# Stage 4 attention of a perceiver-style decoder: scores, transposes and values in another order, normalisation moved to the output copy, and spare products in the waits of the norms

## The reference, cut to what matters

```python
q = (query @ Wq + bq).reshape(b, -1, H, HD).transpose(0, 2, 1, 3)     # b=8, 64 tokens, H=16, HD=32
k = (key @ Wk + bk).reshape(b, -1, H, HD).transpose(0, 2, 1, 3)       # key = value = ctx, 1601 rows
v = (value @ Wv + bv).reshape(b, -1, H, HD).transpose(0, 2, 1, 3)
scores = jnp.einsum('bhsd,bhtd->bhst', q, k) / sqrt(HD)
scores = jnp.where(keep[None, None], scores, neg)
w = jax.nn.softmax(scores, axis=-1)
w = jnp.where(keep[None, None], w, 0)
out = jnp.einsum('bhst,bhtd->bhsd', w, v)
return out.transpose(0, 2, 1, 3).reshape(b, -1, D) @ Wo + bo
```

## Time and profile before

| what | us |
|---|---|
| median of 3 runs | 3006.52 (3006.23 to 3009.16) |
| the profiled execution, its own time | 3007.62 |
| its span in the trace | 3005.7 |
| PE busy in that span | 2785.7 (93%) |
| DVE busy | 1232.9 (41%) |
| ACT busy | 987.7 (33%) |

### The profile page before, as it was taken

One profiled execution on the slowest core, in us unless ns is written; L12 is line 12 of the kernel. 1 busy time (PEld: TensorE's weight loads), 2 busy tenths in 40 slices (PEclk: granted clock), 3 DMA queues, 4 the chain that ended last, 5 costly groups with the idle time before them and its releaser, 6 DMA issues.

```text
span 3005.7 us, 40740 instructions
## 1 busy us (share of the span) xinstructions
PE 2785.7 (93%) x17928; PEld 1966.6 (65%) x17928; DVE 1232.9 (41%) x1873; ACT 987.7 (33%) x1484; POOL 287.2 (10%) x278
## 2 busy tenths in 40 slices
PE   8979999998899799999999969999999999988698
PEld 3347346456587478888888838778778878853433
DVE  4364343447731633333333342442443343344612
ACT  3243113125342344344334412432332332331210
POOL 1110110221012000000000011011011001000000
PEclk9999999998899999999999979999999999999799
DMA  8964994951021132222222210100100100013198
GB/s 358 356 235 151 377 355 174 382 187 52 15 98 56 57 113 99 98 98 98 98 98 94 92 70 22 42 18 34 47 26 22 47 26 22 26 64 126 43 396 359
DMA packets 61967, 385.52 MB, mean 128 GB/s; under 512 B 6192, under 2 KB 10544, under 8 KB 32352
## 3 DMA queue, kind: packets, MB, share of 16 engines
q1 hardware_dynamic: 27072, 190.58, 16.7%
q0 software_dynamic: 29776, 188.15, 16.3%
q10 hardware_dynamic: 4944, 4.20, 0.4%
HBM read 377.64 MB, written 5.26 MB: 127 GB/s over the span
## 4 chain that ended last, share of the span: by engine, by line
PE 77%; DVE 8%; DMA 3%; ACT 3%; issue 1%; POOL 1%; ACTq 0%; DVEq 0%; POOLq 0%
PE PS L431 11%; PE PS L432 11%; PE PS L433 11%; PE PS L310 4%; PE PS L1859 3%; PE PS L1840 3%; PE PS L631 3%; PE PS L1823 3%; PE PS L1842 3%; PE PS L1841 3%; PE PS L1824 3%; PE PS L1825 3%; PE PS L1876 3%; PE PS L604 2%; DMA PR<-in_ctxN 2%; DVE T L1329 2%
## 5 line engine op out<-in xcount | busy, mean ns | idle before, releaser
L431 PE MATMUL PS<-X_high,W_high 128*128 128x512 f32 x576 | 226.5, 393 | 11.0 <-DVE X_low L1240 11.0
L431 PE MATMUL PS<-H_high,W_high 128*128 128x512 f32 x576 | 224.8, 390 | 2.1 <-DVE rstd L1545 2.1
L432 PE MATMUL PS<-X_low,W_high 128*128 128x512 f32 x576 | 225.8, 392 | 0.0
L433 PE MATMUL PS<-X_high,W_part 128*128 128x512 f32 x576 | 225.5, 392 | 0.0
L432 PE MATMUL PS<-H_low,W_high 128*128 128x512 f32 x576 | 224.8, 390 | 0.0
L433 PE MATMUL PS<-H_high,W_part 128*128 128x512 f32 x576 | 224.6, 390 | 0.0
L1187 DVE TENSOR_TENSOR W_part<-ring,W_high 128x2048 fp32r<-128x2048 f32 x63 | 147.1, 2334 | 185.0 <-ACT W_high L1183 185.0
L1183 ACT ACTIVATE W_high<-ring 128x2048 fp32r<-128x2048 f32 x72 | 137.0, 1914 | 252.4 <-PE PS L433 252.4
L2025 DVE TENSOR_TENSOR RB<-PS,rows 128x512 f32<-128x512 f32 x104 | 71.9, 691 | 312.8 <-PE PS L1842 312.8
L1226 DVE TENSOR_TENSOR H_low<-T,H_high 128x512 fp32r<-128x512 f32 x144 | 99.4, 691 | 210.5 <-ACT H_high L1213 210.5
L1955 ACT ACTIVATE RC<-PS,vec 128x384 f32<-128x384 f32 (+2 forms) x128 | 76.3, 596 | 322.4 <-PE PS L1825 322.4
(11 more groups left out here) (380 smaller groups left out, 5490.5 us busy)
## 6 DMA issues: line engine op xcount, KB each, us to landing
ring<-in_experts SPq DMA_DIRECT2D x83, 1024.0 KB, 4.8
ring<-in_tiles SPq DMA_DIRECT2D x39, 1024.0 KB, 4.9
RC<-in_ctxN POOLq DMA_DIRECT2D x24, 1536.0 KB, 12.3
RA<-in_ctxT POOLq DMA_DIRECT2D x20, 1536.0 KB, 7.2
T<-in_ctxN POOLq DMA_DIRECT2D x24, 1024.0 KB, 16.2
RA<-in_ctxT POOLq DMA_DIRECT2D x12, 1666.0 KB, 14.1
RB<-in_ctxT POOLq DMA_DIRECT2D x12, 1666.0 KB, 15.6
RB<-in_ctxT POOLq DMA_DIRECT2D x12, 1536.0 KB, 10.6
```

The lines of the kernel that those rows point to most:

```text
L431: pe.matmul(ps, a, xh, start=start, stop=False)
L432: pe.matmul(ps, a, xl, start=False, stop=False)
L433: return pe.matmul(ps, b, xh, start=False, stop=stop)
```

## The change

It has two parts. In stage 4: the scores of a group take 4 x 448 columns that overlap (0 to 447, 768 to 1215; 320 to 767, 1216 to 1663) rather than 4 x 416; the keys of the second half are made with the key weights' columns turned by 64 (`wrapped_high`, `wrapped_low`, bias `bk4s`) and a second copy of the queries turned likewise (`QSB`), so that the two products of a head over two column ranges lie in different strips of rows. Which heads form a group changes, and the rows of Wo are permuted to match. `normalise` is gone; `inverse` writes reciprocals of the sums, repeated 32 times, into a 128 x 128 tile, which one product with `FOLD` (L1939) spreads into PSUM behind the last two transposed blocks; the copy of the group's output multiplies by it and by `flag`. Transposes are cut into 7 pieces (6 of 4 blocks, one of 2 blocks and the product). Scores, transposes and values stand in another order, and three of the 8 units of the next batch's first keys stand inside groups 2 and 3. In the norms from stage 2 on: `turn_over` issues bf16 products of 128 x 512 whose result nobody reads, 5 behind the mean, 5 (14 in one place) behind the squares, and 10 or 22 behind the last spread.

```diff
+        def turn_over(pe, at, n, k=7):
+            pe.wait_ge(*at.done("idb"))
+            if bank_reader.get(k):
+                pe.wait_ge(*at.done(bank_reader[k]))
+            for _ in range(n):
+                pe.matmul(bank(k), idb[:, :], constants, start=True, stop=True)
...
-        def norm_pe(pe, at, tag, x, after):
+        def norm_pe(pe, at, tag, x, after, n=10):
 
             norm_mean(pe, at, tag, x, after)
+            turn_over(pe, at, 5)
             norm_squares(pe, at, tag, TS[5])
+            turn_over(pe, at, 5)
             norm_scale(pe, at, tag)
+            turn_over(pe, at, n)
...
+                for p in (0, 1):
+                    if g or h:
+                        pe.wait_ge(*at.done(f"{N}.m{g}.0.{p}" if h else f"{N}.m{g - 1}.1.{p}"))
+                    for late, m in enumerate(scored(h)):
+                        for u in (0, 1):
+                            block = 4 * (g // 2) + 2 * u + g % 2
+                            place = (block - late) % 8
+                            r = slice(place % 2 * S + p * HD, place % 2 * S + (p + 1) * HD)
+                            mm = pe.matmul(PS[u * S:(u + 1) * S, 2 * p + late, 0:SW], (QSB if late else QS)[r, place // 2, :], KT[r, place // 2, m:m + SW],
+                                           start=True, stop=True)
+                    mm.then_inc(*at.step(f"{N}.S{g}.{h}.{p}"))
...
                 for g in range(KC):
-                    transposes(b, g, 0, 0)
-                    transposes(b, g, 0, 1)
-                    transposes(b, g, 1, 0)
-                    transposes(b, g, 1, 1)
-                    if g + 1 < KC:
+                    if g in (1, 2):
                         scores(b, g + 1, 1)
+                    transposes(b, g, 0, 1, 2, 3)
                     values(b, g, 0)
-                    transposes(b, g, 2, 0)
-                    transposes(b, g, 2, 1)
-                    values(b, g, 1)
-                    transposes(b, g, 3, 0)
-                    transposes(b, g, 3, 1)
-                    values(b, g, 2)
-                    if g + 2 < KC:
-                        scores(b, g + 2, 0)
-                    if g + 1 == KC and b + 1 < B:
-                        keys(b + 1, 0)
-                    values(b, g, 3)
+                    if g == 0:
+                        scores(b, 1, 1)
+                    elif g == 1:
+                        scores(b, 3, 0)
+                    elif b + 1 < B:
+                        keys(b + 1, 0, range(g - 2, g - 1))
+                    transposes(b, g, 4, 5, 6)
+                    if g == 3 and b + 1 < B:
+                        keys(b + 1, 0, range(2, 3))
+                    values(b, g, 1, 2, 3)
+                    if g == 0:
+                        scores(b, 2, 0)
+                if b + 1 < B:
+                    keys(b + 1, 0, range(3, 8))
...
-            def normalise(b, g, q):
-                x, sm = prob[2 * (g % 2) + q], total4[g % 2][q]
-                dve.wait_ge(*at.done(f"s4.{b}.exp{g}.{q}"))
-                dve.reciprocal(sm, sm).then_inc(*at.step())
-                dve.wait_ge(*at.own())
-                dve.tensor_scalar(x, x, sm, flag, ALU.mult, ALU.mult).then_inc(*at.step(f"s4.{b}.p{g}.{q}"))
+            def inverse(b, g):
+                dve.wait_ge(*at.done(f"s4.{b}.exp{g}.1"))
...
+                for u in (0, 1):
+                    r = slice(u * S, (u + 1) * S)
+                    dve.reciprocal(INV[r, :, u, :], total4[g % 2][r, :].unsqueeze(2).broadcast_to([S, 2, HD])).then_inc(*at.step(f"s4.{b}.inv{g}"))
```

More of the change, by code:

```diff
@@ L1648, in s3_pe @@
             linear_pe(pe, at, "s3.o", [("s3.wo", O3)], (0, 1, 2, 3), range(KC), ["s3.at.O3.out"])
-            norm_pe(pe, at, "s3.ln1", X3, [f"s3.o.{c}.out" for c in range(KC)])
+            norm_pe(pe, at, "s3.ln1", X3, [f"s3.o.{c}.out" for c in range(KC)], 22)
             def gates_turned():
@@ new lines, in transposes @@
+            def transposes(b, g, *pieces):
+                N = f"s4.{b}"
+                for i in pieces:
+                    s = g * PN + i
+                    if s >= 3:
+                        due = [f"{N}.t{s - 3}.out"]
+                    elif s < 2:
+                        due = [f"{N}.V1.{HALF[1][1] - 1 - s}.out"]
+                    else:
+                        due = [f"s4.{b - 1}.t{BLOCKS - 2}.out"] if b else []
+                    if i < 2:
+                        due.append(f"{N}.exp{g}.{i}")
+                    if i == PN - 1:
+                        due.append(f"{N}.inv{g}")
+                    for name in at.last(*due) if due else []:
+                        pe.wait_ge(*name)
+                    for j, (m, q) in enumerate(PIECES[i]):
+                        mm = pe.transpose(PS[:, TBANK[s % 3], j * P:(j + 1) * P], prob[2 * (g % 2) + q][:, m * P:(m + 1) * P], C["ident"])
+                    if i == PN - 1:
+                        mm = pe.matmul(PS[:, TBANK[s % 3], 2 * P:2 * P + S], kconv[:, 2:4, :].rearrange("p a m -> p (a m)"), FOLD, start=True, stop=True)
+                    mm.then_inc(*at.step(f"{N}.t{s}"))
@@ new lines, in values @@
+            def values(b, g, *ks):
+                N = f"s4.{b}"
+                for k in ks:
+                    if k == 0 and (g or b):
+                        pe.wait_ge(*at.done(f"{N}.o{g - 1}.out" if g else f"s4.{b - 1}.o{KC - 1}.out"))
+                    for due in at.last(*(f"{N}.t{g * PN + i}.out" for i in VNEEDS[k])):
+                        pe.wait_ge(*due)
+                    for m in VPARTS[k]:
+                        for a in range(G):
+                            q, r = divmod(a, 2)
+                            f = head4(g, q, r) * HD
+                            i, j = TURNED_AT[m, q]
+                            mm = pe.matmul(PS[a * HD:(a + 1) * HD, 6, 0:S], VT[:, m, f:f + HD], turned_at(g, i)[:, j * P + r * S:j * P + (r + 1) * S],
+                                           start=(m == VPARTS[0][0]), stop=(m == VPARTS[-1][-1]))
+                    mm.then_inc(*at.step(f"{N}.v{g}.{k}"))
@@ L1947, in s4_act, with keys_out @@
             act.wait_ge(*at.done("s4.flag"))
[L1949 removed]
+            def keys_out(b, h, ns=range(8)):
                 N = f"s4.{b}"
                 m0, mt = HALF[h]
[L1952 removed]
+                for n in ns:
                     c0, c1 = KCOLS[h][n % 2]
@@ L2070, in s4_dve @@
-                out(b, KC - 1)
+                maxima(b, 0, 1)
+                values_in(b, 1, range(4, HALF[1][1]))
+                maxima(b, 1, 0)
+                for g in range(KC):
+                    if g in (1, 2):
+                        maxima(b, g + 1, 1)
+                    if g == 3:
+                        turn_out(b, g * PN + 1)
+                        turn_out(b, g * PN + 3)
+                    else:
+                        turn_out(b, g * PN + 3)
+                    inverse(b, g)
+                    if g == 0:
+                        maxima(b, 1, 1)
+                    elif g == 1:
+                        maxima(b, 3, 0)
+                    elif g == 3:
+                        turn_out(b, g * PN + 5)
+                    out(b, g)
+                    if g == 0:
+                        maxima(b, 2, 0)
```

244 lines of the change are left out of this document (127 added, 117 removed).

## The result

The changed kernel takes 2925.5 us in the median of four runs (2919.3 to 2929.2) beside 3007.8 us for the kernel before on the same chip: a ratio of 0.9724, 95% interval 0.9704 to 0.9744, so 82 us less. The prediction was 2926 us. Each experiment is compared with the kernel before on its own chip, 3005 to 3007 us there.

What follows compares the result with a forecast made beforehand. PE, busy 93% of the span, was taken as the bound, in stage 4's groups by its work and switches. 3007.6 - 61 (stage 4) - 20 (norms) = 2926.6, the runs' median 1.1 lower: forecast 2926 us, 8-in-10 range 2902 to 2968.

Steps and rivals of the forecast that it cites:

- A set of scores runs eight at a time: Stage 4's scores: eight products in eight array places take 0.75 us a set, where a set took 1.41 before.
- The dense part: Stage 4's stretch outside the groups, 59.2 us a batch: three sets of scores in it save 2.0 us.
- Waits: PE idle in stage 4's groups: 3.3 us a batch left, 2.3 of it ahead of group 2's second set.
- Switches: PE changing between transposes, scores and values, 0.15 us each: 21 a batch for 34, 1.9 us less.
- The clock in the groups: Stage 4: the clock no longer falls to 0.50 in group 3 of every second batch, winning 0.75 us a batch.
- The rival: Clock falls in every batch's groups, in the wait ahead of group 2's second scores: 23 us, 2949; chance 0.08.
- The norms: Fill holds the clock in eight norms, so sums and the products behind them run warm: 20 us less.
- five products that start cold: Norms: five products behind the sums start at half clock; with fill they start warm, 11 us less.
- Nothing is won: Rival: PE's 30.6 busy us are all work, switches free, FOLD and 448 columns eat the rest: 3006; chance 0.03.
- neighbours wait: Rival: score products sharing a strip of rows wait, a set takes 3.75 us: 3103; chance 0.03.
- four at a time: Rival: scores stay at four at once, 1.50 us a set, stage 4 wins only 27 us: 2959; chance 0.17.
- the ring: Stage 4's groups before: the chain scores, maxima, exp, normalise, transposes is nearly as long as PE's work and switches.

Runs made afterwards that it cites:

- e3: Changed kernel with a set's eight score products in four places of the array, issued in two rounds of four: 2970.7 us, ratio 0.9883.
- e1: Changed kernel without the bf16 fill products in the norms, stage 4 as changed: 2944.1 us, ratio 0.9793.
- e4: Changed kernel with `normalise`'s two DVE passes back ahead of each group's transposes: 2981.7 us, ratio 0.9918.
- e7: Changed kernel with four bf16 products of 448 columns between group 2's two sets of scores: 2922.8 us, ratio 0.9722.
- e2: Kernel before with only the norms' bf16 fill products added, stage 4 untouched: 2994.9 us, ratio 0.9958.
- e10: Changed kernel with three more fills: ahead of stage 2's output product, stage 3's convolution and its last norm's sums: 2934.1 us, ratio 0.9760.
- e6: Changed kernel with four units of next keys inside the groups rather than three, one in each gap of group 3: 2925.1 us, ratio 0.9733.
- e8: Changed kernel with three waits at stage 4's edges removed by order (mask preparation, first keys, fetch of Wo's weights): 2923.0 us, ratio 0.9723.
- e11: Changed kernel with the edits of e6, e7 and e8 together: 2900.0 us, ratio 0.9650.
- e12: e11 with the three fills of e10 added: 2904.9 us, ratio 0.9661.

## Why the prediction was right, point by point

- **A set of scores runs eight at a time**, 0.75 us and 0.90 with its switch: measured 0.94 and, with four places, 1.66 (predicted 1.65). e3 shows that 43 us of the gain hang on this term.
- **The rule on strips of rows.** The next product's weights share the strip of the one before in every pair of a set, and a set took 0.94 us, not 3.9. The Trainium skill, "TensorE: Matmul & The Clock Gate", Part 3, says that a weight load overlaps running products only when its row group differs; by that rule the kernel would have been slower than before. Page and measurement differ, and the measurement decides. The 0.75 us that the prediction also draws from that part's 10.6 times doesn't follow from it: 16 records of 0.375 us are 6.0 us, which by 10.6 would be 0.57, and by half as much, an estimate for half as many places, 1.1. The 0.75 rests on the 0.375 us a record alone.
- **FOLD** 0.3 us: 0.27. **The dense part** 2.0 us: 2.3. **Groups** 28.9 us: 28.2.
- **Waits** 3.3 us: in the list of idle time 1.70, and 1.0 more inside the rows of sets that wait half-way; together 2.7. The wait ahead of group 2's second set was forecast at 1.4 and measured at 1.06.
- **Switches** 1.9 us a batch less: the groups' sum comes out, but no run changed the number of switches alone, so their share is argued from rows and not shown.
- **Stage 4 in all**: 61 us predicted; 66 by the two traces; without the fill (e1) 63 by the runs and 58 by the trace from stage 1's end on.
- **The clock in the groups** is where the prediction's step failed in part. I took back all 0.75 us a batch; it no longer falls in group 3, but falls in group 1 in two of seven batches, for 1.6 and 3.1 us. The rival had it there in every batch, as it came about in e4, where the wait is 1.15 us. e7 shows place and price.
- **The norms**: 20 us predicted; 11.5 by subtraction in the trace; by the runs 12 alone (e2) and 19 beside stage 4's part (e1), 6 of these by fewer falls in stage 4's groups. The mis-sized term is "five products that start cold (11 us)" with all cold sums: several of these follow a wait without fill (stage 2's output product, the convolution, the sums of stage 3's last norm, the spread in stage 4's), and stayed cold. e10 adds that a cold start needn't cost anything: with the convolution warm the stretch up to the next norm was no shorter. That the sum came out right to 1 us is in part luck: stage 4 won 5 us more than predicted, the norms 8 to 9 less, and in the profiled execution stage 1 was 7 us short. By the medians of its two measurements the change is worth 77 to 82 us for the 81 predicted.
- "Nothing is won", "neighbours wait" and "four at a time" fall with the 0.94 us of a set; e3 shows what the last would have cost. That the ring was "nearly as long" as PE's work was right: e4 shows PE waiting for `normalise` in every batch once the scores are short.

Open: why the clock falls in some batches and not in others that are the same code and lengths. In the changed kernel's two executions it fell in the same two batches, though stage 1 ended 5.2 us later in one; both reached batch 0 1161.7 us behind stage 1's end. e10 reached it 1.1 us later, and the clock fell in four batches; e1, e6 and e8 had more falls as well. The time from stage 1's end to the groups seems to matter, but no run moved that alone.

## What to carry to other kernels

Small products can run all at once when each has a place of its own in the array, even if neighbours share a strip of rows: count places, not neighbours. Products in different strips of rows wrote different banks in all these runs; none varied that. Price a step both ways when two bounds are near each other: taking one away wins only up to the other. Where the clock falls behind a wait, fill the wait with products into columns that nobody reads any more. A fill that must first wait for its bank cost more than it brought, and a few clock falls of 1.6 to 3.1 us hid the gain of a better order (e6). And split the trace at marks that unchanged code ends with, before reading a difference of a few us.

## What the runs showed of the hardware that was not expected

- Stage 1, the same instructions in all fourteen profiled executions, ended between 700.9 and 709.8 us. That is as much as the runs of one kernel spread.
- DVE instructions of 1.02 and 1.03 us took 3.56 and 7.38 us beside POOL's (e8), ending 0.9 us behind them. The Trainium skill, "SBUF — State Buffer", "Who interferes with whom", says that DVE in a two-port mode and GpSimd share a port pair, and whoever comes second blocks fully; by that rule the delay is what is left of POOL's instruction, and the trace agrees: 2.5 and 6.4 us of delay beside 2.7 and 6.5 us that POOL's instructions had left. Which mode DVE ran in no view shows.
- The clock fell behind a wait of 1.06 us with 0.94 us of scores on either side, in some batches only, and in every batch behind one of 1.15 us in e4. It didn't fall with four bf16 products in that wait (e7, e11, e12), nor with scores four at a time behind a wait of 1.19 us (e3).
